# Second layer: probabilities and the next x transposed by row halves of the array in one group a step

## What is computed

```python
xn = layer_norm(x, norm_w, norm_b)
q = (xn @ q_w + q_b).reshape(Bx, Tx, H, -1)        # H = 16 heads of 32
k = (xn @ k_w + k_b).reshape(Bx, Tx, H, -1)
att = jnp.einsum('bnhl,bmhl->bnmh', q, k)
att = jax.nn.softmax(att + (1.0 - mask) * -1000000.0, axis=2)
v = ((xn @ v_w + v_b) * src_mask[:, :, None]).reshape(Bx, Tx, H, -1)
y = jnp.einsum('bnmh,bmhl->bnhl', att, v).reshape(Bx, Tx, Dx)
h = layer_norm(y, sb_norm_w, sb_norm_b) * (1.0 + scale) + shift
return x + jax.nn.silu(h) @ out_w + out_b
```

## Time and profile before

| | us |
|---|---|
| three runs | 2091.98, 2092.11, 2093.65 (median 2092.11) |
| the profiled execution | 2092.2 |
| its span, first to last instruction | 2090.3 |
| mean granted TensorE clock | 0.998 |

### The profile page before, as it was taken

The page is one execution under the profiler, slowest core; times in us unless marked ns, Lnnn a source line. Parts: engine busy times, 40 slices in busy tenths (PEclk is TensorE's granted clock), DMA queues, the critical chain, the costliest instruction groups (busy, mean ns, idle before and its releaser), DMA issues.

```text
span 2090.3 us, 48294 instructions
## 1 busy us (share of the span) xinstructions
PE 2065.4 (99%) x17499; PEld 1818.4 (87%) x17499; DVE 1396.2 (67%) x2995; ACT 1151.3 (55%) x3806; POOL 579.0 (28%) x861
## 2 busy tenths in 40 slices
PE   7999999999999999999999999999999999999997
PEld 5888888888888888888898989898898989898986
DVE  6877777777777777776665556665565655566655
ACT  4333333334323433354677777777777777777775
POOL 4323332333233322334222222222222222222220
PEclk9999999999999999999999999999999999999999
DMA  7211011100011001102210101101010101011000
GB/s 234 93 40 40 25 35 40 40 30 35 35 40 38 27 35 40 40 26 77 67 36 25 35 25 35 40 20 40 25 35 25 35 25 35 25 35 40 20 31 21
DMA packets 52165, 86.43 MB, mean 41 GB/s; under 512 B 5668, under 2 KB 14566, under 8 KB 52135
## 3 DMA queue, kind: packets, MB, share of 16 engines
q1 hardware_dynamic: 52118, 86.03, 12.1%
q10 hardware_dynamic: 16, 0.00, 0.0%
HBM read 52.32 MB, written 33.69 MB: 41 GB/s over the span
## 4 chain that ended last, share of the span: by engine, by line
PE 96%; DVE 2%; ACT 1%; DMA 0%; issue 0%; SPq 0%; POOL 0%; POOLq 0%; DVEq 0%; ACTq 0%
PE bank L538 14%; PE bank L539 14%; PE bank L540 14%; PE bank L547 9%; PE bank L548 9%; PE bank L549 9%; PE bank L1742 5%; PE bank L1755 3%; PE bank L1732 3%; PE bank L1129 3%; PE bank L1117 2%; PE bank L1014 1%; PE bank L1038 1%; PE bank L1692 1%; PE bank L1764 1%; PE bank L1042 1%
## 5 line engine op out<-in xcount | busy, mean ns | idle before, releaser
L547 PE MATMUL bank<-xT_hi,w_hi 128*128 128x256 f32 x1536 | 448.0, 292 | 0.8 <-DVE xT_lo L379 0.8
L548 PE MATMUL bank<-xT_lo,w_hi 128*128 128x256 f32 x1536 | 438.8, 286 | 0.0
L549 PE MATMUL bank<-xT_hi,w_lo 128*128 128x256 f32 x1536 | 436.1, 284 | 0.0
L1561 ACT ACTIVATE heads<-bank,top 128x128 f32<-128x128 f32 x1024 | 358.6, 404 | 88.1 <-DVE top L1354 87.9
L538 PE MATMUL bank<-w_hi,xT_hi 128*128 128x512 f32 x768 | 305.4, 398 | 0.4 <-DVE bias_all L396 0.4
L540 PE MATMUL bank<-w_lo,xT_hi 128*128 128x512 f32 x768 | 301.2, 392 | 0.0
L539 PE MATMUL bank<-w_hi,xT_lo 128*128 128x512 f32 x768 | 300.2, 391 | 0.0
L547 PEld LDWEIGHTS bank<-xT_hi,w_hi 128*128 128x128 f32 x1536 | 292.2, 190 | 8.6 <-issue 3.8
L548 PEld LDWEIGHTS bank<-xT_lo,w_hi 128*128 128x128 f32 x1536 | 292.4, 190 | 0.5 <-issue 0.5
L549 PEld LDWEIGHTS bank<-xT_hi,w_lo 128*128 128x128 f32 x1536 | 292.8, 191 | 0.0
L1354 DVE TENSOR_REDUCE top<-bank 128x4 f32<-128x512 f32 x256 | 162.8, 678 | 180.9 <-PE bank L1732 180.9
(11 more groups left out here) (203 smaller groups left out, 4048.6 us busy)
## 6 DMA issues: line engine op xcount, KB each, us to landing
xr<-in_x SPq DMA_DIRECT2D x32, 512.0 KB, 3.4
x_between_layers<-ends SPq DMA_DIRECT2D x64, 256.0 KB, 2.0
xr<-x_between_layers SPq DMA_DIRECT2D x32, 512.0 KB, 4.1
out<-ends SPq DMA_DIRECT2D x64, 256.0 KB, 2.1
store<-in_L_cond_W_emb SPq DMA_DIRECT2D x4, 1024.0 KB, 11.8
store<-in_L_cond_emb_w SPq DMA_DIRECT2D x3, 1024.0 KB, 8.0
mask_rows<-mask_parts SPq DMA_DIRECT2D x128, 2.0 KB
heads<-in_L_cond_Wk SPq DMA_DIRECT2D x1, 1024.0 KB, 7.6
```

Of the source, the lines that this page charges most:

```text
L547: yield nc.tensor.matmul(dst, w_hi[:, m, c, fs], a_hi[:, c], start=(first and c == 0), stop=False)
L548: yield nc.tensor.matmul(dst, w_hi[:, m, c, fs], a_lo[:, c], start=False, stop=False)
L549: yield nc.tensor.matmul(dst, w_lo[:, m, c, fs], a_hi[:, c], start=False, stop=(last and c == C - 1))
L1561: last = nc.scalar.activation(prob[:, a, c, :], ps[a][:, c * P:(c + 1) * P], ACT.Exp, bias=top[:, b, h:h + 1], accum_out=total[:, b, h:h + 1])
```

## The change

A new helper transposes blocks by row halves. Each 128 x 128 block becomes two transposes of 64 rows x 128 columns with 64 moving columns. Half 0 sits in the upper 64 rows of the array and half 1 in the lower 64, and each half writes its own PSUM bank:

```diff
+def turn_halves(nc, ident, banks, blocks):
+    half = P // 2
+    for n, src in enumerate(blocks):
+        for r in range(2):
+            rows = slice(half * r, half * r + half)
+            last = nc.tensor.transpose(banks[r][:, half * n:half * n + half], src[rows, :], ident[rows, rows],
+                                       tile_position=(half * r, 0))
+    return last
```

`prob_turned` (16 blocks) and `x_turned` (8 blocks) use it. Banks are given out anew, and in step 0 all 24 blocks come in one group, ahead of `value_rows(i, 1)`:

```diff
-    Y_BANK, Z_BANK, O_BANK = 4, 7, 6
-    QK_BANKS, V_BANKS, X_BANKS = (5, 6), (5, 6), (5, 7)
+    Z_BANK, EMB_BANK = 4, 4
+    Y_BANKS, O_BANKS = (5, 7), (6, 4)
+    QK_BANKS, V_BANKS, X_BANKS = (7, 6), (5, 5), (7, 6)
...
         def step0(i):
...
             run(value_rows(i, 0))
-            z_transposed(i - 1, 1)
-            prob_turned(i, 0, (0, 1))
+            z_turned = z_transposed(i - 1, 1)
+            run(islice(z_turned, C - 1))
+            pe.wait_ge(s["prob"], seq(PAIR * C, i, C))
+            pe.wait_ge(s["xn"], seq(PAIR, i + 1, PAIR))
+            pe.wait_ge(s["y"], seq(PAIR, i - 1, PAIR))
             pe.wait_ge(s["out"], seq(PAIR, i - 1, 1))
+            run(z_turned)
+            prob_turned()
+            x_turned()
+            pe.wait_ge(s["v"], seq(PAIR, i, 1))
             run(value_rows(i, 1))
-            prob_turned(i, 0, (2, 3))
-            pe.wait_ge(s["v"], seq(PAIR, i, 1))
-            x_transposed(i + 1, 0)
             pe.wait_ge(s["g"], seq(PAIR, i - 1, PAIR))
-            x_transposed(i + 1, 1)
-            pe.wait_ge(s["v"], seq(PAIR, i, PAIR))
             run(out_rows(i - 1, 1))
-            mixed(i, 0, False)
+            mixed(i, 0, Y_BANKS[0])
...
         def step1(i, first):
...
+            pe.wait_ge(s["prob"], seq(PAIR * C, i, PAIR * C))
             pe.wait_ge(s["k"], seq(2, i + 1, 1))
             run(projected(i + 1, Q, (0, 1)))
-            prob_turned(i, 1, range(HC))
+            prob_turned()
...
             run(projected(i + 1, Q, (2, 3)))
-            mixed(i, 1, first)
+            pe.wait_ge(s["q"], seq(2, i + 1, 1))
+            mixed(i, 1, Y_BANKS[1])
```

On ACT and DVE the copies out of these banks keep their number and place, and change their pattern: a bank now holds one row half of 8 blocks. The first of ACT's x copies also waits for `value_rows(i, 1)`, since it overwrites what those read:

```diff
+        def x_high(pair, r):
+            if r == 0:
+                act.wait_ge(s["v_ps"], seq(PAIR, pair - 1, PAIR))
+            act.wait_ge(s["xT_ps"], seq(PAIR, pair, PAIR))
...
-                nc.scalar.activation(prob_T[:, a], ps[a][:, :].rearrange("p (c t) -> p c t", c=C),
+                first, r = a // 2 * 2, a % 2
+                nc.scalar.activation(prob_T[:, first:first + 2, :, HALF * r:HALF * r + HALF],
+                                     ps[a][:, :].rearrange("p (n c t) -> p n c t", n=2, c=C),
```

More of the change, by code:

```diff
@@ L1192, in v_banks @@
     def v_banks(pair):
-        if isinstance(pair, int) and pair in (0, LAST):
-            return LAST_V_BANKS if pair else FIRST_V_BANKS
-        return V_BANKS
+        return FIRST_V_BANKS if isinstance(pair, int) and pair == 0 else V_BANKS
     def sync(sp):
@@ L1332, in norm, with first_x_low, x_low @@
                                         ALU.mult).then_inc(s["xn"], 1)
-        def x_low(pair, b, banks=X_BANKS):
-            dve.wait_ge(s["xT_hi"], seq(PAIR, pair, b + 1))
-            nc.vector.tensor_tensor(xT_lo[:, :, b, :], ps[banks[b]][:, :].rearrange("p (c t) -> p c t", c=C),
+        def first_x_low(b, bank):
+            dve.wait_ge(s["xT_hi"], b + 1)
+            nc.vector.tensor_tensor(xT_lo[:, :, b, :], ps[bank][:, :].rearrange("p (c t) -> p c t", c=C),
                                     f32(xT_hi[:, :, b, :]), ALU.subtract).then_inc(s["xT_lo"], 1)
+        def x_low(pair, r):
+            rows = slice(HALF * r, HALF * r + HALF)
+            dve.wait_ge(s["xT_hi"], seq(PAIR, pair, r + 1))
+            nc.vector.tensor_tensor(xT_lo[:, :, :, rows], ps[X_BANKS[r]][:, :].rearrange("p (c b t) -> p c b t", c=C, b=PAIR),
+                                    f32(xT_hi[:, :, :, rows]), ALU.subtract).then_inc(s["xT_lo"], 1)
         def keys_out(pair, chunks):
@@ L1487, in vector @@
         for b in range(PAIR):
-            x_low(0, b, (2, 3))
+            first_x_low(b, 2 + b)
         yield
@@ L1536, in scalar, with first_x_high @@
     def scalar(act):
-        def x_high(pair, b, banks=X_BANKS):
-            act.wait_ge(s["xT_ps"], seq(PAIR, pair, b + 1))
-            nc.scalar.activation(xT_hi[:, :, b, :], ps[banks[b]][:, :].rearrange("p (c t) -> p c t", c=C),
+        def first_x_high(b, bank):
+            act.wait_ge(s["xT_ps"], b + 1)
+            nc.scalar.activation(xT_hi[:, :, b, :], ps[bank][:, :].rearrange("p (c t) -> p c t", c=C),
+                                 ACT.Copy).then_inc(s["xT_hi"], 1)
+        def x_high(pair, r):
+            if r == 0:
+                act.wait_ge(s["v_ps"], seq(PAIR, pair - 1, PAIR))
+            act.wait_ge(s["xT_ps"], seq(PAIR, pair, PAIR))
+            nc.scalar.activation(xT_hi[:, :, :, HALF * r:HALF * r + HALF],
+                                 ps[X_BANKS[r]][:, :].rearrange("p (c b t) -> p c b t", c=C, b=PAIR),
                                  ACT.Copy).then_inc(s["xT_hi"], 1)
@@ L1567, in prob_out, with last_prob_out, copy_yT @@
                 act.wait_ge(s["pT_ps"], seq(PAIR * C, i, b * C + a + 1))
+                first, r = a // 2 * 2, a % 2
+                nc.scalar.activation(prob_T[:, first:first + 2, :, HALF * r:HALF * r + HALF],
+                                     ps[a][:, :].rearrange("p (n c t) -> p n c t", n=2, c=C),
+                                     ACT.Copy).then_inc(s["pT"], 1)
+        def last_prob_out(some):
+            for a in some:
+                act.wait_ge(s["pT_ps"], seq(PAIR * C, LAST, C + a + 1))
                 nc.scalar.activation(prob_T[:, a], ps[a][:, :].rearrange("p (c t) -> p c t", c=C),
                                      ACT.Copy).then_inc(s["pT"], 1)
-        def copy_yT(prev, b, bank=Y_BANK):
+        def copy_yT(prev, b, bank=None):
+            bank = Y_BANKS[b] if bank is None else bank
             act.wait_ge(s["yT_ps"], seq(PAIR, prev, b + 1))
@@ L1681, in tensor, with first_x_turned, x_turned, out_rows @@
     def tensor(pe):
-        def x_transposed(pair, b, banks=X_BANKS):
-            pe.wait_ge(s["xn"], seq(PAIR, pair, b + 1))
+        def first_x_turned(b, bank):
+            pe.wait_ge(s["xn"], b + 1)
             for c in range(C):
-                last = nc.tensor.transpose(ps[banks[b]][:, c * P:(c + 1) * P], xn[:, b, c * P:(c + 1) * P], ident[:])
+                last = nc.tensor.transpose(ps[bank][:, c * P:(c + 1) * P], xn[:, b, c * P:(c + 1) * P], ident[:])
             last.then_inc(s["xT_ps"], 1)
+        def x_turned():
+            banks = [ps[n] for n in X_BANKS]
+            turn_halves(nc, ident, banks, [xn[:, b, c * P:(c + 1) * P] for c in range(C) for b in range(PAIR)])\
+                .then_inc(s["xT_ps"], PAIR)
         def z_transposed(prev, b, bank=Z_BANK):
             pe.wait_ge(s["z"], seq(PAIR, prev, b + 1))
+            last = None
             for c in range(C):
                 last = nc.tensor.transpose(ps[bank][:, c * P:(c + 1) * P], z[:, b, c * P:(c + 1) * P], ident[:])
-            last.then_inc(s["z_ps"], 1)
-        def out_rows(prev, b, bank=O_BANK):
+                if c == C - 1:
+                    last.then_inc(s["z_ps"], 1)
+                yield
+        def out_rows(prev, b, bank=None):
+            bank = O_BANKS[b] if bank is None else bank
             pe.wait_ge(s["h_lo"], seq(PAIR, prev, b + 1))
@@ L1735, in scores, with last_prob_turned @@
                         last.then_inc(s["s_ps"], 1)
-        def prob_turned(i, b, some, banks=range(HC)):
+        def last_prob_turned(b, some, banks=range(HC)):
             for a in some:
-                pe.wait_ge(s["prob"], seq(PAIR * C, i, b * C + a + 1))
+                pe.wait_ge(s["prob"], seq(PAIR * C, LAST, b * C + a + 1))
                 for c in range(C):
@@ L1743, in prob_turned, with mixed @@
                 last.then_inc(s["pT_ps"], 1)
[L1745 to L1751, removed]
+        def prob_turned():
+            for a in (0, 2):
+                turn_halves(nc, ident, (ps[a], ps[a + 1]), [prob[:, a + n, c, :] for n in range(2) for c in range(C)])\
+                    .then_inc(s["pT_ps"], 2)
+        def mixed(i, b, bank):
+            pe.wait_ge(s["v"], seq(PAIR, i, PAIR if bank == V_BANKS[1] else b + 1))
             pe.wait_ge(s["pT"], seq(PAIR * C, i, C * (b + 1)))
@@ L1758, in mixed, with turned @@
             last.then_inc(s["yT_ps"], 1)
-        def turned(prev, b, bank=Y_BANK):
+        def turned(prev, b, bank=None):
+            bank = Y_BANKS[b] if bank is None else bank
             pe.wait_ge(s["yT"], seq(PAIR, prev, b + 1))
@@ L1829, in first_step0 @@
             pe.wait_ge(s0["x1"], PAIR * NP)
-            x_transposed(1, 0)
-            x_transposed(1, 1)
             pe.wait_ge(s["v"], PAIR)
-            products = emb.products(pe, ps[O_BANK])
+            pe.wait_ge(s["xn"], 2 * PAIR)
+            x_turned()
+            products = emb.products(pe, ps[EMB_BANK])
             run(islice(products, 3 * emb.KE // 2))
```

(39 more changed lines are left out.)

21 lines of the change are left out of this document (12 added, 9 removed).

## The result

The changed kernel takes 2120.35 us (median of 4 runs, 2118.6 to 2120.7) against 2092.05 us: a ratio of 1.0131 with a 95% interval of 1.0117 to 1.0144. It is slower by 28.3 us, where 19.4 were forecast. The profiled execution took 2120.18 us, its span 2118.3, at a granted clock of 0.998 like before, so the time is not in the clock.

A forecast was written before the change was run, and what follows sets the result against it. PE's stream was taken to bound the kernel. Step 0 +1.07 us and step 1 -0.39 make +0.68 a pair, +20.4 over 30 pairs; with -1.0 for pair 0, 2092.2 + 19.4 = 2111.6 us, range 2090 to 2126.

The forecast's parts named there:

- A block at 0.062 us: PE's transposes: two 64-row halves run in the time of one, 0.062 us a block, saving 0.047 us per block.
- the weight load sets the pace: Rival on PE's half transposes: the load isn't halved, a block stays at 0.109 us, 2168 us in all; chance 0.06.
- the halves don't overlap: Rival on PE's half transposes: one runs after the other, 0.124 us a block, 2186 us in all; chance 0.04.
- A group at 0.34 us: Each group of halves on PE changes the tiling twice: 0.15 us to enter, 0.19 to leave.
- free tiling: Rival: changing the tiling around a group of halves costs nothing, 2091 us, no measurable change; chance 0.07.
- streaming alone: Rival: loads hide under the other half's stream, 0.0545 us a block, nothing for a group, 2082 us; chance 0.09.
- Step 1 shorter by 0.39 us: Step 1 of a pair: 0.75 us saved on 16 blocks, less 0.34 for the group and 0.02 for the exponentials.
- The lost cover, 1.60 us of idle PE: Step 0: transposes no longer cover the wait for DVE's h_lo behind the last value matmul; PE idles 1.60 us.
- The wake from a wait, 0.05 us: PE resumes 0.05 us after a release, used in step 0 at the exponentials and at h_lo.
- Pair 0, -1.0 us: First pair, no stall: 24 blocks save 1.1 us in step 0, about half lost to the exponentials; step 1 saves 0.4.

The follow-up runs named there:

- the run with one more group: Changed kernel with step 1's 16 blocks in two groups of 8, six query matmuls between them: 2130.2 us.
- The exchange on DVE: Changed kernel with DVE making h_lo ahead of the second v in step 0: 2070.3 us; the same exchange in the kernel before: 2092.55 us.
- series of 8 and of 24: Changed kernel with upper halves, then lower, not in turn: per series of 8, 2147.3 us; per whole group (24 in step 0, 16 in step 1), 2185.8 us.

## Why the prediction was right, and where it fell short

The direction, the cause and its place were right, and the range held the time. Step by step:

- *A block at 0.062 us.* Right. In the profile after, 32 halves take 0.99 us to the last one's start; the first distance is longer, as in the earlier trace rows, so the other 14 distances share about 0.88 us. The rival in which the weight load sets the pace is refuted by the row of the loads: 32 loads of 128 columns start in 1.07 - 0.14 = 0.93 us, two every 0.062 us. That the halves don't overlap is refuted too, since 32 would then take 2.0 us. The Trainium skill, page "TensorE: Matmul & The Clock Gate", section "LDWEIGHTS (loading the stationary operand)", gives 107 ns for a load of 128 columns; the loads of this trace don't agree.
- *A group at 0.34 us.* 0.32 in the run with one more group. Right within 0.03. With it, and with 0.062 us a block, the two rivals of free tiling and of streaming alone fall.
- *Step 1 shorter by 0.39 us.* 0.40 in the mean of the pairs. The key matmuls follow each other every 0.120 us in the trace before, not every 0.118, so PE comes to the exponentials a little later than the sum has it; nothing hangs on that.
- *The lost cover, 1.60 us of idle PE.* 1.54 in the list of waits, by the profile's own way of counting, and 1.92 us from start to start for 1.83. The exchange on DVE changes nothing else and takes it away, and in the kernel before it is worth nothing, so the cause is shown.
- *The wake from a wait, 0.05 us.* This is the term that was mis-sized. It came from the earlier trace rows, where a single semaphore is waited for. In the changed step 0 both late waits share their place with further ones, so two instructions that only wait stand ahead of the load at the exponentials and one at h_lo, and the wake is 0.22 and 0.11 us. With the satisfied waits moved away step 0 takes 18.27 us, and 18.25 was forecast (17.18 + 1.07). That is 0.23 of the 0.25 us by which step 0 was short. All pairs of the loop together came 7.2 us over the sum.
- *Pair 0, -1.0 us.* From its first scores to those of pair 1 it is 29.2 us instead of 29.8: -0.6. Step 0 got 0.55 us shorter, as forecast, but step 1 only 0.05: there PE waits 0.22 us for ACT's copies of the probabilities ahead of `mixed`, which the sum had as covered.
- Another 1.2 us lie ahead of the second layer: its first scores start at 1003.65 instead of 1002.43, and the loop of the first layer is unchanged. The traces of this series have that start between 1002.2 and 1004.8 whatever the kernel; what makes it vary was not looked into.

7.2, 0.4 and 1.2, less 0.2 us from pair 31 on, are the 8.6 us between 2111.6 and the profiled 2120.2. The range held the time with 6 us to spare.

## What to carry to other kernels

When a block of work is moved or made faster, ask what it was covering: here 16 transposes hid the path from a result over two operations of another engine back to PE, and moving them ahead cost more (65 us, with the waits of the new order) than making them faster gained (36 us). Before giving the move up, look at the order on the other engine: h_lo didn't need the result that stood ahead of it, and one exchanged line turned +28 us into -23. Put a wait that can be late alone and directly at its instruction, and those that are long satisfied some instructions earlier: in the changed kernel that was worth 7 us.

## What the runs showed of the hardware

- Two row halves of PE's array work at once on 64-row transposes: 32 halves issued in turn take the 0.99 us that 16 take in series.
- Matmuls in different rows of the array start out of program order, but only over a short distance: a lower half started with three upper ones still ahead of it, in series of 8 and of 24 alike (1469.78, and 1487.54 against 1487.60, 1487.66 and 1487.72). The Trainium skill, page "TensorE: Matmul & The Clock Gate", section "The mechanism", says that matmuls keep program order in start and end; the starts at 1487.54 and 1487.60 don't agree with it.
- On PE, an instruction that only waits and stands between a late release and the weight load costs about 0.08 us, even if its own condition is long satisfied: from the release to the load it is 0.05 us with none, 0.11 with one and 0.22 with two. In step 0 that was 0.23 us with the stall and 0.22 without it, some 7 us in 30 pairs.
